# Pad rows of the expert areas written during the token loop, and the last shared tiles begun in the last expert steps

## The reference

```python
x = x + jnp.tanh(g_xattn[0]) * xattn(layernorm(x), ctx)
t = layernorm(x).reshape(-1, 256)                        # 2048 tokens
scores = jax.nn.sigmoid(t @ W_gate_router)
_, sel = jax.lax.top_k(scores + expert_bias, 2)
top = take(scores, sel) / (sum over the two + 1e-20)
shared = silu(t @ Wg_s) * (t @ Wu_s) @ Wd_s
routed[n] = silu(t @ Wg[e]) * (t @ Wu[e]) @ Wd[e]        # e: the two chosen experts
x = x + jnp.tanh(g_ffn[0]) * (shared + sum(top * routed))
```

## Time and profile before

| | us |
|---|---|
| median of three runs | 332.17 |
| lowest, highest | 331.71, 333.2 |
| the profiled execution, its own time | 331.99 |
| its span in the trace | 330.2 |
| mean granted TensorE clock, share of full | 0.946 |
| PE busy | 279.2 (85%) |
| DVE busy | 248.5 (75%) |
| POOL busy | 160.6 (49%) |
| ACT busy | 153.6 (47%) |

### The profile page before, as it was taken

One profiled execution on the slowest core, in us unless ns is written; L12 is line 12 of the kernel. 1 busy time (PEld: TensorE's weight loads), 2 busy tenths in 40 slices (PEclk: granted clock), 3 DMA queues, 4 the chain that ended last, 5 costly groups with the idle time before them and its releaser, 6 DMA issues.

```text
span 330.2 us, 6385 instructions
## 1 busy us (share of the span) xinstructions
PE 279.2 (85%) x1724; PEld 251.2 (76%) x1725; DVE 248.5 (75%) x708; ACT 153.6 (47%) x387; POOL 160.6 (49%) x208
## 2 busy tenths in 40 slices
PE   3968979999989989969968779089799999999680
PEld 2958768999979978959957667078699999999560
DVE  1696898999999998869967755028877777777666
ACT  1362455555555654635433365024456555555310
POOL 7022023355556888884788505705644443444400
PEclk9997999999999999998979999659999999999877
DMA  5792003011111232342003992232344334334668
GB/s 189 264 338 64 0 0 97 1 50 49 50 49 45 77 113 75 96 129 66 32 34 118 319 287 75 81 93 84 96 114 124 101 103 125 118 112 128 203 222 287
DMA packets 33628, 38.01 MB, mean 115 GB/s; under 512 B 3816, under 2 KB 30274, under 8 KB 33602
## 3 DMA queue, kind: packets, MB, share of 16 engines
q1 hardware_dynamic: 28018, 27.13, 27.7%
q0 software_dynamic: 3408, 8.46, 7.5%
q10 hardware_dynamic: 2176, 2.10, 1.9%
HBM read 21.67 MB, written 16.93 MB: 117 GB/s over the span
## 4 chain that ended last, share of the span: by engine, by line
PE 43%; DVE 18%; POOL 12%; issue 12%; DMA 6%; SPq 5%; ACT 2%; DVEq 0%; POOLq 0%; ACTq 0%
POOL rows_dram L556 6%; PE bank L1232 5%; PE scores_ps L1232 4%; PE bank L1233 4%; PE bank L1234 4%; PE scores_ps L1233 4%; PE scores_ps L1234 4%; DMA x_sb<-in_x_dram 3%; PE bank L1389 3%; POOL probs L585 2%; PE bank L1218 2%; DVE pT_lo L1032 2%; DVE row_sum L1037 2%; DMA routed_dram<-probs,sct_idx 2%; DVE probs L1061 2%
## 5 line engine op out<-in xcount | busy, mean ns | idle before, releaser
L638 POOL DMA_INDIRECT routed_dram<-probs,sct_idx x39 | 38.6, 991 | 56.2 <-ACT probs L804 55.1
L585 POOL TENSOR_TENSOR probs<-probs,row_inv 128x1024 f32<-128x1024 f32 x16 | 30.5, 1906 | 33.9 <-DVE row_inv L1041 33.9
L556 POOL DMA_INDIRECT rows_dram<-xn,slot_i x32 | 31.9, 997 | 20.1 <-DMA rows_dram<-pad_rows 11.5
L1232 PE MATMUL bank<-AB_hi,pT_hi 128*128 128x256 f32 x128 | 38.5, 301 | 0.0
L1234 PE MATMUL bank<-AB_hi,pT_lo 128*128 128x256 f32 x128 | 37.0, 289 | 0.0
L1233 PE MATMUL bank<-AB_lo,pT_hi 128*128 128x256 f32 x128 | 37.0, 289 | 0.0
L1232 PE MATMUL scores_ps<-AB_hi,xnT_hi 128*128 128x512 f32 x64 | 25.9, 404 | 3.4 <-DVE xnT_lo L1021 3.4
L1120 DVE TENSOR_TENSOR xnT_lo<-bank,xnT_hi 128x256 fp32r<-128x256 f32 x39 | 16.5, 424 | 14.9 <-ACT xnT_hi L789 13.7
L719 ACT ACTIVATE probs<-probs 128x1024 f32<-128x1024 f32 x16 | 16.9, 1058 | 19.0 <-DVE probs L1061 19.0
L1232 PEld LDWEIGHTS bank<-AB_hi,pT_hi 128*128 128x128 f32 x128 | 25.6, 200 | 0.0
L1233 PEld LDWEIGHTS bank<-AB_lo,pT_hi 128*128 128x128 f32 x128 | 25.6, 200 | 0.0
(11 more groups left out here) (224 smaller groups left out, 864.2 us busy)
## 6 DMA issues: line engine op xcount, KB each, us to landing
rows_dram<-pad_rows SPq DMA_DIRECT2D x8, 650.0 KB, 10.6
probs<-rows_dram SPq DMA_DIRECT2D x30, 130.0 KB, 2.2
x_sb<-in_x_dram SPq DMA_DIRECT2D x2, 1024.0 KB, 9.7
AB_free<-routed_dram SPq DMA_DIRECT2D x4, 512.0 KB, 6.3
AB_free<-routed_dram SPq DMA_DIRECT2D x8, 256.0 KB, 4.8
out_dram<-x_sb ACTq DMA_DIRECT2D x8, 256.0 KB, 2.2
raw_buf<-in_L_ffn_Wg_dram SPq DMA_DIRECT2D x8, 192.0 KB, 2.5
raw_buf<-in_L_ffn_Wu_dram SPq DMA_DIRECT2D x8, 192.0 KB, 2.7
```

What stands on the lines that cost most here:

```text
L556: nc.gpsimd.indirect_dma_start(rows_dram[:, :], bass.IndirectOffsetOnAxis(ap=slot_i[:, t, k:k + 1], axis=0), xn2[:, t % KEEP, :], None).th ...
L585: nc.gpsimd.tensor_tensor(pr, pr, row_inv[:, :].unsqueeze(2).to_broadcast([P, H, KV]), ALU.mult).then_inc(norm_done, 1)
L638: nc.gpsimd.indirect_dma_start(routed_dram[:, :], bass.IndirectOffsetOnAxis(ap=sct_idx[(k - 2) % (2 * RING)][:, 0:1], axis=0), y_sb[ks][:, ...
L1232: nc.tensor.matmul(out_ap, a_hi, b_hi, start=first, stop=False)
```

## The change

Areas have 16 tiles instead of 17. `put_pads` and the counting for it on PE and DVE are gone. In their place every row of every area gets a pad before any token's row is put: the first six tiles of each area by eight transfers (780 KB each) that SP issues behind its first loads, tile 6 to 15 of all areas by ten transfers of eight tiles (1040 KB each), one behind each of the later weight loads. POOL waits before tile 0's puts for the first eight transfers (`filled[0]`), and before tile t's puts, t from 6, for one more. The wait for the pads ahead of batch 4 is gone. SP's wait before the gathers stays for the one pad tile behind the areas.

Of the shared tiles 11 to 15 the first three are begun in expert steps j = 39 and 40, in which PE has no new slot. Each of the five has its own PSUM bank, so that `late_down` no longer waits for readers, and PE waits for the last copy but one ahead of the last of them alone.

```diff
-REGION = T + 1
+REGION = T
-COUNTED = 3
-PAD_ROWS = T - BATCHES[COUNTED][1] + 1
+FIRST = 6
...
+        lhT_ps = [pT_ps[z % 2] if z < NB else bank[2 + (z - NB) % 2] for z in range(T)]
+        tail_ps = [bank[4], scores_ps[:, 0:512], scores_ps[:, 512:1024], bank[5], bank[1]]
...
-        def put_pads(eng):
...
+        def fill_first(eng):
+
+            eng.wait_ge(pad_ready, 3)
+            eng.dma_start(rows_dram[PAD_TILE * P:(PAD_TILE + 1) * P, :], pad_rows[:, :]).then_inc(pads_put, 16)
+            for e in range(E):
+                area = rows_dram[e * REGION * P:(e * REGION + FIRST) * P, :]
+                eng.dma_start(area.rearrange("(p r) d -> p r d", r=FIRST),
+                              pad_rows[:, :].unsqueeze(1).to_broadcast([P, FIRST, ROW])).then_inc(filled[0], 16)
+
+        def fill_next(eng, s):
+
+            areas = rows_dram[0:PAD_TILE * P, :].rearrange("(e s p) d -> s p e d", s=REGION, p=P)
+            eng.dma_start(areas[FIRST - 1 + s], pad_rows[:, :].unsqueeze(1).to_broadcast([P, E, ROW])).then_inc(filled[s], 16)
...
+            fill_first(sp)
             sp.wait_ge(B_done, HP)
...
+                if e >= 2:
+                    fill_next(sp, e - 1)
...
+                fill_next(sp, E - 1 + n)
-            put_pads(sp)
...
+                if t == 0:
+                    pool.wait_ge(filled[0], 16 * E)
+                if t >= FIRST:
+                    pool.wait_ge(filled[t - FIRST + 1], 16)
...
-            pool.wait_ge(pads_put, 16 * (E + 1))
             put_batch(4)
...
+                if isinstance(j, int) and j == SLOT_TILES:        # ACT
+                    late_hidden(NB)
+                    late_hidden(NB + 1)
+                if isinstance(j, int) and j == SLOT_TILES + 1:
+                    late_hidden(NB + 2)
...
+                if isinstance(j, int) and j == SLOT_TILES:        # PE
+                    late_transpose(NB)
+                    late_transpose(NB + 1)
+                if isinstance(j, int) and j == SLOT_TILES + 1:
+                    late_down(NB)
+                    late_transpose(NB + 2)
+                    late_down(NB + 1)
...
-            pe.wait_ge(ycopy_done, SLOT_TILES)
-            for z in range(NB, T):
-                late_transpose(z)
-                if z > NB:
-                    late_down(z - 1)
-            late_down(T - 1)
+            late_transpose(NB + 3)
+            late_down(NB + 2)
+            late_transpose(NB + 4)
+            late_down(NB + 3)
+            pe.wait_ge(ycopy_done, SLOT_TILES - 1)
+            late_down(NB + 4)
```

More of the change, by code:

```diff
@@ L159, in flamingo_layer @@
         tile_row = sb("tile_row", [1, Q + RING], I32)
-        pad_row = sb("pad_row", [1, E], I32)
         low_turns = sb("low_turns", [1, RING], I32)
@@ L209, in flamingo_layer @@
         cmp_ps = route[:, 160:160 + Q * E].rearrange("p (j e) -> p j e", e=E)
-        lhT_ps = pT_ps
-        late_ps = [scores_ps[:, 0:512], scores_ps[:, 512:1024], att_ps]
+        lhT_ps = [pT_ps[z % 2] if z < NB else bank[2 + (z - NB) % 2] for z in range(T)]
+        tail_ps = [bank[4], scores_ps[:, 0:512], scores_ps[:, 512:1024], bank[5], bank[1]]
+        late_ps = [[scores_ps[:, 0:512], scores_ps[:, 512:1024], att_ps][z % 3] if z < NB else tail_ps[z - NB] for z in range(T)]
         gT_ps = [bank[3], bank[2]]
@@ L240, in flamingo_layer @@
         count_ps_done = sem("count_ps_done")
-        pads_ps_done = sem("pads_ps_done")
-        pad_row_done = sem("pad_row_done")
         pad_ready = sem("pad_ready")
@@ L245, in flamingo_layer @@
         pads_put = sem("pads_put")
+        filled = [sem(f"filled{s}") for s in range(REGION - FIRST + 1)]
         tile_row_done = sem("tile_row_done")
@@ L460, in _ @@
                 sp.wait_ge(rows_put[r], 16 * TOPK * T // KEEP)
-            sp.wait_ge(pads_put, 16 * (E + 1))
+            sp.wait_ge(pads_put, 16)
             def expert_step(j, k, i):
@@ L708, in late_hidden @@
                 after(act, late_done, z - 1)
-                nc.scalar.activation(lhT[z % 2][:, :, :], lhT_ps[z % 2][0:FH, 0:2 * P].rearrange("p (k s) -> p k s", k=2),
+                nc.scalar.activation(lhT[z % 2][:, :, :], lhT_ps[z][0:FH, 0:2 * P].rearrange("p (k s) -> p k s", k=2),
                                      ACT.Copy).then_inc(lhT_done, 1)
@@ L767, in late_copy @@
                 act.wait_ge(late_done, z + 1)
-                nc.scalar.activation(late_out[:, z, :], late_ps[z % 3][:, 0:D], ACT.Copy).then_inc(late_read, 1)
+                nc.scalar.activation(late_out[:, z, :], late_ps[z][:, 0:D], ACT.Copy).then_inc(late_read, 1)
             gates_of_shared(T - 2)
@@ L806, in _ @@
             expert_loop(act, expert_step)
-            for z in range(NB, T):
+            for z in range(NB + 3, T):
                 late_hidden(z)
@@ L1001, in late_add @@
                 dve.wait_ge(plane0_added, z + 1)
-                nc.vector.tensor_tensor(x_sb[:, z, :], late_ps[z % 3][:, 0:D], x_sb[:, z, :], ALU.add).then_inc(late_read, 1)
+                nc.vector.tensor_tensor(x_sb[:, z, :], late_ps[z][:, 0:D], x_sb[:, z, :], ALU.add).then_inc(late_read, 1)
             def second_norm(t):
@@ L1045, in step @@
                     if z + 2 == t:
-                        if b == COUNTED:
-                            pad_rows_at()
                         place(b)
@@ L1257, in late_transpose @@
                 for k in range(2):
-                    mm = nc.tensor.transpose(lhT_ps[z % 2][0:FH, k * P:(k + 1) * P], late_hid[:, z, k * FH:(k + 1) * FH], ident[:, :])
+                    mm = nc.tensor.transpose(lhT_ps[z][0:FH, k * P:(k + 1) * P], late_hid[:, z, k * FH:(k + 1) * FH], ident[:, :])
                 mm.then_inc(lhT_ps_done, 1)
@@ L1262, in late_down @@
                 pe.wait_ge(lhT_done, z + 1)
-                after(pe, late_read, z - 2)
+                after(pe, late_read, min(z, NB) - 2)
                 for k in range(2):
-                    mm = nc.tensor.matmul(late_ps[z % 3][:, 0:D], lhT[z % 2][:, k, :], Wds[:, k, :], start=(k == 0), stop=(k == 1))
+                    mm = nc.tensor.matmul(late_ps[z][:, 0:D], lhT[z % 2][:, k, :], Wds[:, k, :], start=(k == 0), stop=(k == 1))
                 mm.then_inc(late_done, 1)
@@ L1328, in step @@
                         rank(b)
-                        if b == COUNTED:
-                            count(range(*BATCHES[b]), pads_ps_done)
                 if inside(v):
```

5 lines of the change are left out of this document (removed).

## The result

| | median us | runs | lowest, highest |
|---|---|---|---|
| before | 331.94 | 4 | 331.52, 333.2 |
| after | 322.9 | 4 | 321.94, 323.89 |

The ratio is 0.9722 (95% interval 0.968 to 0.9763): 9.0 us faster. The forecast was 320.3, with 318.2 to 323.6 as its range. The profiled execution of the changed kernel took 323.89 us, the longest of the four, for a span of 322.1.

The account below looks back on a forecast made before the run. The prediction took the relay of pads, puts, gather and PE before the expert loop as the bound, with ACT's copy next. Terms -9.25 - 2.5 + 0.3 - 0.2 = -11.65 us gave 320.3 us, range 318.2 to 323.6.

Parts of the forecast that it names:

- Term 1: Before the expert loop: without the wait for pads PE starts at 206.3 instead of 215.54, held by ACT's copy; -9.25 us.
- Term 2: First expert steps: with a short hole before the loop PE's clock stays full instead of half; -2.5 us, between 0 and 3.56.
- the clock falls all the same: Rival at the expert loop's start: PE's clock still falls, term 2 shrinks to 1.0, time 321.8 us; chance 0.15.
- Term 3: Early pad writes in SP's queue: nearly all covered, x's second half may be held up slightly; +0.3 us, up to 3.6.
- Term 4: Kernel's end: shared tiles begun earlier gain little because transfers set the end; -0.2 us, between -1.9 and +1.2.
- DVE's way: Rival at the kernel's end: DVE's work alone decides, term 4 becomes -1.9, time 318.6 us; chance 0.1.
- The slow side: First pads written too slowly, delaying the token loop; whole gain gone at 128 GB/s, 335 us at 120 GB/s; chance 0.03.
- the first stage: Rival at the kernel's start: early pads hold up x's second half, term 3 up to 3.6, time up to 323.6; chance 0.1.
- the one with 0.04: Rival: something else, for instance a late put, holds the expert loop; with 2 us, time 322.3; chance 0.04.

Follow-up runs that it names:

- the counts put back: Three counting matmuls of token step 14 back in the changed kernel, DVE waiting for them: 321.22 us, ratio 0.9605; once more 324.14 us, beside the changed kernel's 323.88.
- filler: Changed kernel plus 18, 18 and 8 identity transposes on PE in steps 11, 13, 14: 321.31 us against 323.88; later 321.95 against 322.75.
- the first comparison: One chip, kernel before 334.88 us, changed kernel not run; counting matmuls put back 321.22 us, early pads without late tiles 322.33 us.
- the filler in the kernel before: Kernel before plus identity transposes on PE after the last shared tile before the expert loop: 80 of them 335.37 us, ratio 1.0015; 100 of them 333.35 us, ratio 0.9938.
- the square: Early pads with and without late tiles, each without and with identity transposes in PE's holes: with late tiles 322.75 and 321.95 us, without 322.61 and 321.65 us.
- the second and the third comparison: Two sets of runs on one chip, each with the kernel before and the changed kernel, which took 323.88 us in the second and 322.75 in the third.

## Why the prediction came out as it did

The profiled execution is 3.55 us above the forecast for it (span 322.1 against 318.55). By stretch: PE's start 3.01 us late (209.31 against 206.3), the loop's start 0.12 better than forecast (8.22 us to the first scatter, 2.62 less than before), first to last scatter 0.67 longer than before (86.08 to 86.75), last scatter to the end 0.08 longer (17.82 against 17.74). 3.01 - 0.12 + 0.67 + 0.08, less the 0.1 that terms 3 and 4 together had added, is 3.54. The median of the four runs is 2.6 above it.

**Term 1, -9.25: right in its mechanism, off in size.** PE started at 206.64 with the counts put back, and at 206.11 with filler. Neither is a clean case: the first had its first addition 0.9 us early (54.03) and lost 1.47 us to a fall of the clock at 98, the second had the late sum of (b) and made up for it in the steps before. Both were released by ACT's copy of tile 10, as forecast. In the first profile it was -6.23. Two sizes were missing.

(a) The prediction's words on it stand in the paragraph of term 3: "the count on PE and the copy on DVE that fall away are a few short instructions; I set one against the other, 0, within 0.3 either way." They cost 1.54 us: without them the hole ahead of step 14's transposes grows from 1.59 to 1.99 us, and the clock falls behind it. The seven against four profiles above carry this, and the three with filler. It is the step of the prediction that failed: the prediction had priced the instructions, not the hole that they filled, though it asked just this question of the hole before the expert loop.

(b) DVE's last slot sum and ACT's copy of a hidden tile beside it, both waiting for PE, came 1.45 us late together. From the last tile's x_sb addition to the slot sum it takes 10.32 to 10.34 us in six profiles and 11.79 to 11.89 in eight. All eight have early pads; so have two of the six (both in the first comparison), and the four with the old pads are all among the short ones, in the first runs, the first comparison and the second. So neither the early pads nor the chip goes with it alone. PE's records show the matmuls at their usual times, as the changed kernel above (the sum's product at 200.41, behind a matmul at 198.68) and the early pads alone show, DVE then PE:

```profile
198.95 0.17 DVE L942 TENSOR_TENSOR hot_val<-hot,bank 128x16 f32<-128x16 f32 x1 [1.62 <-PE bank L1269]
...
198.66 0.25 PE L1269 MATMUL bank<-mask,ones_r 128*128 128x8 f32 x1
```

In the run with the clock at 0.57 from 191 to 195 the sum came at 11.83 as well, though PE's matmul was 0.7 us later: that speaks against PE's work as what sets it. What it is stays open. POOL's puts, which now go on in these microseconds and didn't before, are a difference between the two groups, but the two short ones with early pads have them as well; no run changed the puts by themselves.

In the first profile a third, smaller part comes on top. ACT's copy ended at 208.73 (208.35 + 0.38), 2.57 us later than the forecast had it; PE began at 209.31, released by the gather. The forecast had given the way from the last put's issue to the rows 2.73 + 0.79 + 2.02 = 5.54 us; it took 3.19 to landing, 1.46 to the gather's issue and 2.20 to its landing, 6.85. The middle one is SP's: 1.46 us also with the counts put back and with early pads alone. Without these 1.31 us PE would have been released by ACT's copy, some 0.4 us earlier (an estimate from these rows).

**Term 2, -2.5: right,** -2.62 in the first profile, and tied to the hole by the filler in the kernel before. The rival that the clock falls all the same (0.15) is real: 3 of the 10 profiles with early pads show it, for 1.5 to 1.7 us, with holes no longer (0.67 to 0.77 us) than in those that don't.

**Term 3, +0.3: 0** at DVE's statistics; what stands in its paragraph on the counts is (a) above. Every bound held. The stretches of four microseconds from 28 to 44 moved 286 to 313 GB/s instead of the 240 assumed, the last of the pads landed at 49.56, before the weights were issued at 49.90 (at 53.09 in the profile of the early pads alone), ACT's first split stood at 68.20, and SP's issue of the eight took 18.05 us instead of 12.64 with nobody waiting. The second half of x wasn't late (26.97 against 27.20). The Trainium skill's rule that a queue's descriptors are consumed in ring order on each engine (DMA: Bandwidth & Descriptors, "Queues, rings and completion order") would have given 0, and the trace agrees with it: x's second half was there 0.23 us earlier than before, with 6.39 MB behind it in the queue.

**Term 4, -0.2: 0 to +0.4.** The three forecasts for its parts held: two `late_down` ahead of the last product cost 0.42 us (forecast 0.5), the `late_add` have no holes, transfers decide. Late tiles alone 1.0014, and no difference between the two rows of the square. DVE's way (318.6) is out. The Trainium skill's rule that transfers issued by different engines run on the same 16 DMA engines (same page, "Rules for kernel authors") fits that: a share of 0.91 over the last 12.3 us.

**The slow side** didn't come near: it needed 128 GB/s.

So that the time fell inside the range is in part luck: its upper end was made for the first stage, and the losses are the clock and a late signal in the token loop. Of the rivals the nearest is the one with 0.04, that something else holds the expert loop, each microsecond behind 204.7 + 1.6 costing one: the first rows landed at 209.18, behind ACT's copy, mostly because the last put was issued 3.2 us later than forecast and not because it took long to land.

## What to carry to other kernels

When short instructions are deleted, look at what they stood in: a hole on PE that grows from 1.6 to 2.0 us can cost more than they did (1.5 us, in four of the five profiles that had it), and the same question belongs to every hole, not only to the big one. A wait for a bulk write of constants is best removed by writing everything early, where the queue has slack, even if it is more bytes. Work moved ahead of the last transfers gains nothing when the transfers are at a share of 0.9 behind it, and holding the clock up by filler in one place can be followed by a fall at the next: all three profiles with filler show one, at 191 or at the start of the expert loop.

## What the runs showed of the hardware

- The clock's falls are not a fixed property of a place. With 1.33 us of idleness ahead of 96.35 one execution of the changed kernel had 0.57 from 98 to 102 and lost 1.47 us in that step; another, with 1.34 us ahead of 97.09, had 1.00. The Trainium skill (TensorE: Matmul & The Clock Gate, "The HAM clock gate") says that the monitor runs on its own, not in step with the kernel; that would give just such a lottery, and no run here could set the moment.
- Executions also differ by up to 3.8 us at the first attention addition (54.03 to 57.82), in kernels with and without the change. The changed kernel's medians in the second and the third comparison, on the same chip, lie 1.1 us apart. Differences under 1 us were therefore read from steps within profiles.
- Behind the last scatters, with stores alone left, the changed kernel moved 385 GB/s (316 to 318) and 384 (318 to 320), with loads and stores mixed 225 to 289 (308 to 314).
